# Asking for the image rows of K's split one batch earlier, between the diagonal transfers and G

## The reference

```
q = heads(x @ W_q);  k_t, v_t = heads(text @ W_k), heads(text @ W_v)
probs_t = softmax(q k_t^T * scale);  text_out = probs_t v_t
k_ip, v_ip = heads(ip @ W_k_ip), heads(ip @ W_v_ip)
sem = l2norm(probs_t @ text) . l2norm(ip)          # per head
probs_ip = softmax(q k_ip^T * scale + 0.5 * sem) * spatial_mask
out = (text_out + probs_ip v_ip) @ W_out + b_out + x
```

## Time and profile before

| | us |
|---|---|
| median of 3 runs | 216.6 (216.45 to 216.85) |
| the profiled execution, its own time | 217.86 |
| its span, first to last instruction | 215.8 |
| PE busy | 204.6 (95%) |
| DVE busy | 181.1 (84%) |
| ACT busy | 169.1 (78%) |
| POOL busy | 149.7 (69%) |

### The profile page before, as it was taken

The page is one execution under the profiler, slowest core; times in us unless marked ns, Lnnn a source line. Parts: engine busy times, 40 slices in busy tenths (PEclk is TensorE's granted clock), DMA queues, the critical chain, the costliest instruction groups (busy, mean ns, idle before and its releaser), DMA issues.

```text
span 215.8 us, 6904 instructions
## 1 busy us (share of the span) xinstructions
PE 204.6 (95%) x1589; PEld 191.5 (89%) x1589; DVE 181.1 (84%) x1147; ACT 169.1 (78%) x554; POOL 149.7 (69%) x255
## 2 busy tenths in 40 slices
PE   8898959999997999999999999999999999998984
PEld 8777959999996999999999999999999999987973
DVE  4547758998977798997979797989979798989893
ACT  2639949897986888897988888888969888887721
POOL 2165007379794979879696969698796969697870
PEclk9999999999999999999999999999999999999999
DMA  5524443837364462747365554647364656433101
GB/s 132 146 83 105 109 122 64 225 77 237 58 174 122 120 185 56 208 109 210 95 186 122 163 140 130 170 88 213 68 205 100 189 120 171 94 92 103 46 5 46
DMA packets 41580, 27.45 MB, mean 127 GB/s; under 512 B 8513, under 2 KB 39898, under 8 KB 41562
## 3 DMA queue, kind: packets, MB, share of 16 engines
q1 hardware_dynamic: 40922, 26.81, 47.5%
q10 hardware_dynamic: 640, 0.43, 0.8%
HBM read 10.06 MB, written 1.43 MB: 53 GB/s over the span
## 4 chain that ended last, share of the span: by engine, by line
PE 77%; DVE 5%; POOL 4%; DMA 4%; SPq 4%; ACT 3%; issue 2%; POOLq 0%; DVEq 0%
PE main_ps L974 14%; PE main_ps L976 14%; PE probsT_ps L956 13%; PE pa L946 9%; PE score_ps L1010 7%; DMA k_split<-kip_d 4%; PE pb L1038 4%; PE pb L1050 3%; PE pa L1066 3%; SPq L385 2%; PE main_ps L891 2%; PE pa L1058 2%; POOL rnorm L511 2%; PE pa L886 2%; DVE junk L734 2%
## 5 line engine op out<-in xcount | busy, mean ns | idle before, releaser
L629 ACT ACTIVATE probs<-score_ps,negmax 128x124 f32<-128x124 f32 x320 | 92.5, 401 | 2.0 <-DVE negmax L799 1.9
L734 DVE CUSTOM_DVE_ANT_0 junk<-main_ps,probs 128x124 f32<-128x124 f32 x320 | 77.8, 280 | 2.3 <-PE main_ps L976 2.1
L974 PE MATMUL main_ps<-main_rhs,probsT 124*128 124x137 f32 x320 | 64.2, 281 | 0.7 <-DVE small L736 0.6
L976 PE MATMUL main_ps<-main_rhs,probsT 124*128 124x137 f32 x320 | 63.3, 279 | 0.0
L511 POOL TENSOR_TENSOR rnorm<-clamped,exponent 128x20 f32<-128x20 f32 x15 | 53.2, 3545 | 1.1 <-DVE clamped L719 1.1
L799 DVE TENSOR_REDUCE negmax<-score_ps 128x4 f32<-128x496 f32 x80 | 53.1, 663 | 0.0
L597 ACT ACTIVATE probsT<-probsT_ps 124x512 f32<-124x512 f32 x80 | 49.8, 622 | 3.4 <-PE probsT_ps L956 3.2
L974 PEld LDWEIGHTS main_ps<-main_rhs,probsT 124*128 124x128 f32 x320 | 49.0, 190 | 1.7 <-issue 1.3
L976 PEld LDWEIGHTS main_ps<-main_rhs,probsT 124*128 124x128 f32 x320 | 48.7, 188 | 0.0
L956 PE MATMUL probsT_ps<-ident_sb,probs 128*124 128x128 f32 x320 | 47.9, 272 | 0.0
L956 PEld LDWEIGHTS probsT_ps<-ident_sb,probs 128*124 128x124 f32 x320 | 38.4, 139 | 5.9
(11 more groups left out here) (162 smaller groups left out, 319.2 us busy)
## 6 DMA issues: line engine op xcount, KB each, us to landing
main_rhs<-g_stage SPq DMA_DIRECT2D x16, 660.0 KB, 4.1
vrep<-vip_d SPq DMA_DIRECT2D x13, 320.0 KB, 3.5
k_diag<-k_stack SPq DMA_DIRECT2D x60, 48.0 KB, 2.2
ctxT_sb<-ctxT SPq DMA_DIRECT2D x16, 124.0 KB, 2.7
k_diag<-k_stack SPq DMA_DIRECT2D x60, 32.0 KB, 2.0
xT_sb<-xT SPq DMA_DIRECT2D x16, 80.0 KB, 2.1
xn_sb<-xn SPq DMA_DIRECT2D x15, 80.0 KB, 2.0
out<-out_sb SPq DMA_DIRECT2D x15, 80.0 KB, 3.5
```

The costliest lines, as they stand in the source:

```text
L629: last = act.activation(probs[p][:, h, :], score_ps[(p * G + g) % 2][:, j * TOK:j * TOK + T], ACT.Exp, bias=negmax[p][:, h:h + 1])
L734: dve.tensor_tensor_reduce(junk[:, 2 * r + a, :], u, probs[wb][:, h, :], 1.0, 0.0, ALU.mult, ALU.add, norm2[wb][:, h:h + 1])
L974: pe.matmul(main_ps[r][:, 0:MAIN], probsT[mp][:, 2 * r, :], blk[:, RW - MAIN:RW], start=True, stop=True)
L976: pe.matmul(main_ps[r][:, MAIN:2 * MAIN], probsT[mp][:, 2 * r + 1, :], blk[:, 0:MAIN], start=True, stop=True).then_inc(s_main, 1)
```

## The change

SP's request for the image rows (L355) leaves the start of the window. It now stands behind the eight diagonal transfers and ahead of G, and it asks for the rows of batch b + 2 instead of b + 1; so the rows that PE needs in window b are asked for in window b - 1. The wait for the store of `kip_d` (`s_kip_out`) moves from window 1 to window 0, where SP now meets it between the diagonal transfers and G. The wait on `s_kT` asks for the product of the window's own L1058, which the diagonal transfers in front of it have already waited for by way of `k_stack`. The number of requests (14), their size and PE's waits are the same.

```diff
             def window(b, p, i, w):
                 n = 1 - p
-                if has(w) and has(w, ahead=1) and w != 0:
-
-                    if w == 1:
-                        sp.wait_ge(s_kip_out, 16)
-                    wait(sp, s_kT, b + 1)
-                    sp.dma_start(k_split[T:TOK, :, :, :].rearrange("t h d a -> t (h d a)").bitcast(F32),
-                                 kip_d[bass.ds((b + 1) * NIP, NIP), :]).then_inc(s_kip_in, 16)
                 if has(w) and has(w, ahead=2):
...
                                              [16, 2, KT - odd, TOK])).then_inc((s_kd_even, s_kd_odd)[odd][n], 16)
 
+                    if has(w, ahead=2):
+
+                        if w == 0:
+                            sp.wait_ge(s_kip_out, 16)
+                        wait(sp, s_kT, b + 2)
+                        sp.dma_start(k_split[T:TOK, :, :, :].rearrange("t h d a -> t (h d a)").bitcast(F32),
+                                     kip_d[bass.ds((b + 2) * NIP, NIP), :]).then_inc(s_kip_in, 16)
                     wait(sp, s_main, NPAIR * b)
                     wait(sp, s_gstage, b + 2)
```

## The result

The changed kernel runs at a median of 214.66 us (214.37 to 214.92, 4 runs) against 216.72 for the kernel before beside it. The ratio of the two is 0.9888, with a 95% interval of 0.9851 to 0.9926: 1.1% faster, clear of no change. On the 216.6 from which the forecast started that is 214.2, a gain of 2.4 us where 4.1 were forecast. The profiled execution took 214.37 with a span of 212.3; its predecessor had 217.86 and 215.8, so these two differ by 3.5.

A forecast was written before the change was run, and what follows sets the result against it. PE, busy 95% of the span, was taken as the bound, stalled by late image rows; 2.46 + 1.61 + 0.15 - 0.10 = 4.1 us off the span gave 211.7, hence a 212.5 us median, range 211.8 to 214.4.

The forecast's parts named there:

- the two stalls: L1058 on PE starts 2.46 us late in window 1 and 1.61 in window 4, waiting for the image rows to land.
- The request for batch 2: Issued in window 0 at 24.68 us where G was, it lands in 2.1 us, removing window 1's whole 2.46 us wait.
- still a little late: Rival: rows take 3.3 to 4.4 us even without G, up to 1.1 of window 1's 2.46 stays; typically 213.2; chance 0.14.
- the estimate of 3.9 us: Window 1's rows under high HBM load: 2.1 + 1.8 us, landing at 28.6, with 0.6 us of the wait staying.
- the sum: Whole span: 2.46 + 1.61 + 0.15 - 0.10 = 4.1 us off for windows 1, 4 and 2, less time given back.
- 1.61 for window 4: L1058's late start in window 4, read as rows standing behind G; claimed to go by either bound.
- 0.15 for window 2: L1058's late start in window 2, claimed to go; bounds 0 and 0.15 us, as it could be no DMA wait.
- one fixed difference of 1.26 us: The runs' median of 216.6 lies this far below the profiled 217.86; the same was taken from 213.75, giving 212.5.
- PE's code: Rival: PE waits for instruction fetch at L1058 in windows 1 and 4; 213.7, 214.9 or 216.6 us; chance 0.10.
- the margin of the diagonal transfers that SP issues in window 1: SP is free at 28.81 us and `k_stack` there at 28.96, so they start on time with 0.15 to spare.
- SP and G behind the request: The request holds SP 0.61 to 1.24 us, delaying G, output store and `vip_d`; costed at nothing, covered by margins.

## Why the forecast held, and where its size was off

**What bounds the kernel, and the two stalls.** What L1058 waited for in windows 1 and 4 was the landing, as read. That the rows land late there because they stand behind G is shown for window 1: ahead of G they are on time, and behind G the same lead gains nothing (216.69). For window 4 this reading failed, as said below.

**The request for batch 2.** The value taken, the whole stall, was right, and so, nearly, was the 2.1 us from which it was read: the rows landed in 1.83 us here, and in 1.6 to 2.8 in the six traces with this request ahead of G. No remainder of window 1's wait is left in any of them. The rival "still a little late" is out. The trace does not bear out here what the Trainium skill's page "DMA: Bandwidth & Descriptors", section "Latency and other measured facts", says of an HBM access under high load: by the estimate of 3.9 us that the forecast worked out from it, the rows would have landed at 25.19 + 3.9 = 29.1. They landed at 27.0, and PE starts L1058 at 28.49 without waiting.

**The step that failed: the sum.** It added 1.61 for window 4 and 0.15 for window 2 as if each execution had them, since each was read as the rows standing behind G. But at the same distance behind G, 1.9 us, three other traces have a landing of 2.9 to 3.2 us and no wait in window 4; the 4.39 was that one execution's. The sum was then carried to the median by one fixed difference of 1.26 us, though the profiled execution lay above the median just because of such a wait: the second one, without it, took 216.0. What is left for the median is the wait of window 1, 2.46 and 2.36 in the two traces, and the measured gain is 2.4. The hint was on the table ahead of the forecast: an execution 1.26 slower than the median is likely to hold a wait that the others lack.

**Right within the range, in part by luck.** The 214.2 lies just inside the stated 211.8 to 214.4. The upper end was put there for a window 1 that stays partly late and for PE's code, and neither came; what used the room was a term counted too often.

**What was left out.** Two smaller terms. The stretch at half clock behind window 1's wait, about 1.4 us in 22 of 74 executions, is a gain that the trace of that one execution, at 1.00 throughout, could not show. And the forecast worked out the margin of the diagonal transfers that SP issues in window 1, but not of those that it issues in window 0; these come 0.6 us late or more in some executions, of both kernels, and that held the profiled difference at 3.5.

**SP and G behind the request.** Costed at nothing, and so it is as far as the runs can tell: G landed as late as 6.0 us after its issue with no wait of PE, and moving the request out of G's way gained nothing. The request itself takes SP less than assumed, 0.32 us in the median against 0.88 before.

**PE's code as the reason.** Out for window 1: the wait goes when one DMA request moves, and comes back when the request stands behind G. For window 4 the change proves nothing, since the unchanged kernel had no wait there in its second trace; against code stands that PE started within 0.14 us of the rows' landing. Why that landing was late stays open.

## What to carry to other kernels

A small transfer that is needed soon belongs ahead of a large one on the same queue; here a request behind the large one was as late with a batch of lead as without. Before terms are added up from a profile, set the profiled execution against the median of the runs: if it is slower, one of its waits is likely its own, and a term that hangs on a margin of some tenths is to be counted by how often it occurs. Where the same request lies equally far behind the large transfer in other windows or executions and isn't late there, the large transfer is not the whole reason. Once one stall is gone, look at the next user of the same resource, since PE arrives there earlier: window 2 was late by 0.9 when only window 1's request was moved.

## What the runs showed of the hardware that was not expected

In one trace a wait of PE of 2.34 us was followed by some 3 us at a lower clock (0.50 granted from 32 to 34 us), though PE was busy without a break behind it. In four other traces much the same wait, of 1.75 to 2.21 us, was followed by none of this. By the mean granted clock it comes in 22 of 74 executions of the kernel before, in none of the 34 without the wait, and in none of 12 when PE had dummy matmuls in the wait.

SP's issue of a small request took longer behind the large transfer. The same 5 KB request took SP 0.88 us in the median behind G, 0.32 ahead of G, and 0.27 ahead of the diagonal transfers:

```profile
L387 SPq DMA_DIRECT2D k_split<-kip_d x14: 314/320/481, 25.2 to 175.8; - x14
```

```profile
L373 SPq DMA_DIRECT2D k_split<-kip_d x13: 269/274/325, 28.8 to 169.4; - x13
```

Part of it is only handed on: the issue of the context, which now comes sooner behind G, went from 0.65 to 0.84 us in the median. Likewise, with three 1 KB reads put between G and the request, those took SP 2.10 us together and the request 0.28.
